# Layer-0 attention, second pass: three quantisations of a tile merged into one over 768 columns in two steps

## The chip, the cores and the metric

The kernel runs on one core of a Trainium2 chip. The time is device microseconds of one execution of the whole program; the time before is the median of three runs.

## The reference, cut to what matters

The program computes four pairs of cross-attention and feed-forward blocks on x of shape 8 x 128 x 256. The change lies in the first attention (`_L0_xattn_ref`), and there in the quantisation of the normalised input before its projections:

```
def _div_clamp_fp8(x, scale):
    y = jnp.clip(x.astype(jnp.float32) / scale, -FP8_MAX, FP8_MAX)
    y = y.astype(jnp.bfloat16).astype(jnp.float32)
    return _fp8_roundtrip(y)

def _fp8_linear_pertensor(x, wq, w_scale, in_scale):
    xq = _div_clamp_fp8(x, in_scale)
    return jnp.einsum('bsi,oi->bso', xq * in_scale, wq) * w_scale
```

This attention works in two halves with 16 query heads each. One takes keys and values from the context, the other takes them from x itself. The half on the context needs x quantised once (for its queries). The half on x needs it three times, with three scales: for queries, keys and values. The mixed heads of both halves are quantised in the same way before the output projection.

## The kernel before, in words

`layer0_attention` runs both halves as one march over 16 tiles of 128 tokens: tiles 0 to 7 are the first pass (on the context), tiles 8 to 15 the second pass ("core" in the code). A tile has 8 steps, one for each projection into a bank of 512 columns: k0, q0, k1, q1, v0, q2, v1, q3. The work of an attention unit is spread over later steps. `march` (line 157) walks the steps in order and, in each step, calls the functions of a list in the order of that list, each at its due steps. Each engine has its own list, written out by hand: TensorE, VectorE (lines 643 to 647), ScalarE and GpSimd (lines 826 and 827). No instruction is moved at run time; engines meet through semaphores alone, and each engine issues in order. Due steps of 8 and more fall into the next tile: step 8 of a tile is step 0 of the next.

Rounding to fp8 is split between two engines. VectorE multiplies by the inverse scale (L569, for the input; L600, for the mixed heads), clips (L552), masks the exponent out of the bf16 number (L554) and makes the rounding step from it (L558). GpSimd adds the step (L776) and subtracts it again (L780). For the mixed heads these operations are 128 x 512 (tiles `y16`, `m16`; result `cat`), for the input 128 x 256 (tiles `yq16`, `mq16`; result `xq`). In the profile names stand without their numbers: `l0a_yq` is `yq16`, `l0a_y` is `y16`, `l0a_mq` and `l0a_m` are the rounding steps.

What happens around the change:

- VectorE, odd steps: variance of the heads (L577), `row_max` of the scores (L590), `normalise` (L585, needs GpSimd's L798 of the step before), then `round_mixed`: L600, L552, L554, L558.
- VectorE, even steps: L577, L594, `normalise` where one is due; in step 2 also `add_to_x` (L607, with L150 and L153 in the second pass); then one `quantise` of the next tile in each of the steps 2, 4, 6 (L569, L552, L554, L558). In the first pass only step 2 has one, since only the queries are quantised. Tile 7 is the first in which three are due, tile 14 the last.
- GpSimd, even steps: `round_mixed` (L776, L780 on 512 columns, for the mixed heads of the step before), `rstd` (L798, 128 x 4, power of -0.5), then `quantise` of the same step (L776, L780 on 256 columns), and in tiles 8 and 9 the preparation of output weights (L810). `rstd` is also due in steps 1 and 3.
- TensorE: in each odd step scores (L410) and mix (L427), in each even step the output projection (L438); `turn` (L401) transposes what L585 wrote; `project` comes last in its step (L392 in the second pass, L384 for keys and values of the first). The projection of k0 of a tile is in step 0, that of q0 in step 1, that of v0 in step 4. It waits for `quant_done` of what it reads: one count for queries, two for keys, three for values.

## Time and profile before

| | |
|---|---|
| median of three runs | 1580.31 us (1577.87 to 1581.35) |
| the profiled execution | 1578.64 us, span 1576.8 us |
| mean granted TensorE clock | 0.975 |
| busy, share of the span | TensorE 93%, VectorE 57%, ScalarE 48%, GpSimd 33% |
| the marched tiles of this attention | from about 28 us to 490 us of the span |
| instructions of the input's quantisation | 32 of each of L569, L552, L554, L558, L776, L780 |

Busy shares over the whole span mix many stages. The change touches one stage only, so what counts are the times inside that stage. The timeline of an engine lists its instructions with their start and length; in square brackets stands the idle time in front of one and who ended it.

### The profile page before, as it was taken

What the parts mean: (1) busy time and instruction counts of PE and PEld (TensorE: products, weight loads), DVE (VectorE), ACT (ScalarE), POOL (GpSimd) and SP (SyncE); (2) the same over time, 40 slices, a digit from 0 to 9 for tenths busy, and PEclk for the clock granted to TensorE, in tenths of its full rate; (3) what the DMA queues carried; (4) which work ended last, traced back from release to release, by engine and by line L of the source; (5) the groups of instructions that cost most, each with busy time, mean ns of one, the idle gap of its engine ahead of it and who ended that gap; (6) DMA issues with size and microseconds to landing.
All of it is one profiled execution on the core that took longest, in us unless ns stands there. A gap on an engine that the chain in (4) does not pass through costs nothing. (4 is left out here: it accounts for less than half of the span.)

```text
span 1576.8 us, 22227 instructions
## 1 busy us (share of the span) xinstructions
PE 1465.0 (93%) x6918; PEld 1044.0 (66%) x6918; DVE 905.4 (57%) x1972; ACT 750.5 (48%) x2052; POOL 526.6 (33%) x510
## 2 busy tenths in 40 slices
PE   4889998899999999999999999999866999989998
PEld 2667777777775555557787979676744666665555
DVE  7787879888875342323465454554684555553322
ACT  3778788788884211110343534343454555554210
POOL 2656567877762000000542425221101333321000
PEclk9999999999999999999999999998977999999999
DMA  4211000200004611112100000002131000011120
GB/s 194 67 52 58 8 5 1 92 1 1 1 1 192 227 48 54 54 47 81 64 1 1 1 1 27 1 0 103 54 137 44 1 1 1 0 29 36 48 67 16
DMA packets 21448, 71.63 MB, mean 45 GB/s; under 512 B 3874, under 2 KB 6306, under 8 KB 18260
## 3 DMA queue, kind: packets, MB, share of 16 engines
q1 hardware_dynamic: 13124, 57.34, 9.8%
q10 hardware_dynamic: 8208, 12.87, 2.7%
q8 instruction: 57, 0.93, 0.3%
q14 instruction: 59, 0.48, 0.1%
HBM read 68.98 MB, written 1.22 MB: 45 GB/s over the span
## 5 line engine op out<-in xcount | busy, mean ns | idle before, releaser
L1130 ACT ACTIVATE l0f_silu<-bank 128x512 f32<-128x512 f32 x48 | 28.6, 597 | 199.9 <-PE bank L1054 189.9
L776 POOL TENSOR_TENSOR l0a_stepped<-l0a_y,l0a_m 128x512 f32<-128x512 bf16 x64 | 76.2, 1190 | 107.0 <-DVE l0a_m L558 106.6
L798 POOL TENSOR_TENSOR l0a_head_rstd<-l0a_head_var,all_minus_half 128x4 f32<-128x4 f32 x96 | 102.3, 1068 | 12.8 <-DVE l0a_head_var L577 12.7
L1233 DVE TENSOR_TENSOR l0f_product<-l0f_silu,bank 128x512 f32<-128x512 f32 x48 | 32.9, 687 | 124.3 <-ACT l0f_silu L1130 124.2
L2247 PE MATMUL bank<-l3a_f_xn_t,all_weights_b 128*128 128x512 f32 (+1 forms) x208 | 93.4, 593 | 0.0
L719 ACT ACTIVATE l0a_work<-bank,l0a_neg_max 128x128 f32<-128x128 f32 x256 | 90.5, 370 | 5.5 <-DVE l0a_neg_max L590 5.3
L401 PE MATMUL bank<-all_ident,l0a_work 128*128 128x128 f32 x384 | 61.5, 284 | 31.4 <-DVE l0a_work L585 30.7
L1066 PEld LDWEIGHTS bank<-all_weights_a,l0f_hidden 128*128 128x128 f32 x384 | 72.9, 190 | 25.2 <-issue 17.0
L1670 DVE TENSOR_TENSOR all_weights_a<-bank,all_cols 128x512 f32<-128x512 f32 x64 | 43.9, 690 | 78.7 <-PE bank L1499 46.2
L1066 PE MATMUL bank<-all_weights_a,l0f_hidden 128*128 128x256 f32 x384 | 88.9, 379 | 0.0
L750 ACT ACTIVATE l0a_work<-l0a_work,l0a_row_inv 128x128 f32<-128x128 f32 x256 | 81.9, 400 | 13.3 <-DVE l0a_row_inv L594 13.3
L410 PEld LDWEIGHTS bank<-l0a_k_t,l0a_q_t 128*128 128x128 f32 x512 | 64.4, 192 | 34.6 <-ACT l0a_q_t L705 27.4
L2514 POOL TENSOR_TENSOR l3a_q_scale<-l3a_q_var,all_minus_half 128x4 f32<-128x4 f32 x32 | 32.3, 1010 | 151.6 <-DVE l3a_q_var L2314 151.6
L780 POOL TENSOR_TENSOR l0a_cat<-l0a_stepped,l0a_m 128x512 fp32r<-128x512 f32 x64 | 77.4, 1209 | 10.5 <-issue 6.2
L691 ACT ACTIVATE l0a_squares<-bank 128x512 f32<-128x512 f32 x96 | 57.5, 599 | 44.5 <-DVE l0a_head_var L577 25.0
L585 DVE TENSOR_TENSOR l0a_work<-bank,l0a_head_rstd 128x512 f32<-128x512 f32 x96 | 65.0, 677 | 21.2 <-POOL l0a_head_rstd L798 21.2
L410 PE MATMUL bank<-l0a_k_t,l0a_q_t 128*128 128x128 f32 x512 | 71.8, 283 | 3.5 <-ACT l0a_q_t L705 2.6
L401 PEld LDWEIGHTS bank<-all_ident,l0a_work 128*128 128x128 f32 x384 | 44.1, 143 | 44.7 <-DVE l0a_work L585 41.3
L577 DVE TENSOR_REDUCE l0a_head_var<-l0a_squares 128x4 f32<-128x516 f32 x96 | 65.7, 684 | 10.6 <-ACT l0a_squares L691 10.5
L1853 ACT ACTIVATE l1a_work<-bank,l1a_exp_bias,l1a_q_scale 128x128 f32<-128x128 f32 x128 | 56.9, 455 | 29.6 <-DVE l1a_exp_bias L1736 29.6
L438 PE MATMUL bank<-l0a_wp_high,l0a_cat 128*128 128x256 f32 x256 | 69.7, 305 | 0.2 <-POOL l0a_cat L780 0.2
L427 PE MATMUL bank<-l0a_probs_t,l0a_values 128*128 128x256 f32 x256 | 66.0, 380 | 0.2 <-ACT l0a_probs_t L726 0.2
(417 smaller groups left out, 3798.2 us busy)
## 6 DMA issues: line engine op xcount, KB each, us to landing
l0f_spread<-l0f_weights ACTq DMA_DIRECT2D x32, 192.0 KB, 2.8
all_weights_a<-in_l_w_q SPq DMA_DIRECT2D x2, 2048.0 KB, 14.4
l0f_spread<-l0f_weights ACTq DMA_DIRECT2D x32, 128.0 KB, 2.8
all_weights_b<-in_l_e_gate SPq DMA_DIRECT2D x1, 3072.0 KB, 10.7
all_weights_a<-in_l_e_up SPq DMA_DIRECT2D x4, 768.0 KB, 7.1
all_weights_a<-in_l_e_down SPq DMA_DIRECT2D x1, 3072.0 KB, 15.5
l3a_spread<-l3f_weights SPq DMA_DIRECT2D x10, 256.0 KB, 3.3
all_weights_b<-in_l_w_qx SPq DMA_DIRECT2D x1, 2048.0 KB, 11.4
```

The source lines that it names most:

```text
L401: mm = pe.transpose(turn_bank[:, h * P:(h + 1) * P], norm_rows[:, m % 2, h * P:(h + 1) * P], res.ident[:])
L410: mm = pe.matmul(score_bank[:, h * P:(h + 1) * P], q_t[:, h * P:(h + 1) * P], k_t[:, a // 2, g * P:(g + 1) * P], start=True, stop=True)
L427: mm = pe.matmul(mix_bank[:, half * 2 * P:(half + 1) * 2 * P], values[:, a // 2, g * P:(g + 1) * P], probs_t[:, half * 2 * P:(half + 1) * ...
L438: mm = pe.matmul(out_bank[:, 0:D], cat[:, a % 2, h * P:(h + 1) * P], part[:, a * HU + h, :], start=(a == 0 and h == 0 and n == 0), stop=(a ...
L577: v.tensor_reduce(head_var[:, m % 2, :], squares[:], X, ALU.add).then_inc(var_ready.sem, 1)
L719: done = act.activation(probs[:, a % 2, h * P:(h + 1) * P], score_bank[:, h * P:(h + 1) * P], ACT.Exp, bias=neg_max[:, a, h:h + 1], accum_ ...
L750: done = act.activation(pr, pr, ACT.Copy, scale=row_inv[:, a, h:h + 1])
L776: done = g.tensor_tensor(stepped[:, 0:n], value, step, ALU.add)
L780: return g.tensor_tensor(out, stepped[:, 0:n], step, ALU.subtract)
L798: g.tensor_tensor(head_rstd[:, m % 2, :], head_var[:, m % 2, :], res.minus_half[:, 0:HU], ALU.pow)\
L1066: mm = pe.matmul(down_banks[t // 2][:, (t % 2) * D:(t % 2 + 1) * D], hidden[:, n % 2, t * P:(t + 1) * P], w_down[:, j, :], start=(j == 0 a ...
L2247: mm = pe.matmul(bank[0:m, :], weights[:, c, col:col + m], f_xn_t[:, c, h * HALF:(h + 1) * HALF], start=(c == 0), stop=(c == KC - 1))
```

## The change

On VectorE `quantise` is replaced by three functions. `quant_scale` does the multiplications (three in the second pass, one in the first) in step 2. `quant_clip` clips all columns with one instruction, in step 2 as well. `quant_step` masks and makes the rounding step, each with one instruction, in step 4. GpSimd still rounds in pieces of 256 columns, now in steps 4, 6 and 8, after a wait for the whole tile's rounding steps. The tile `e16` grows from 512 to 768 columns.

```diff
-        e16 = mem.sb("e16", [BANK], BF16)
+        e16 = mem.sb("e16", [3 * D], BF16)
...
-            def quantise(b, i):
-
+            def quant_width(b):
+                return 0 if b == VTS else 3 * D if b >= TILES else D
+
+            def quant_scale(b, _):
                 b += 1
                 core, t = divmod(b, TILES)
-                if b == VTS or (i > 0 and not core):
+                if quant_width(b) == 0:
                     return
                 v.wait_ge(ln_ready, TILES)
-                quant_done.wait(v, quant_done.at(b - 1, i + 1))
-                part = slice(i * D, (i + 1) * D)
-                v.tensor_tensor(yq16[:, part].rearrange("p (c n) -> p c n", c=KC), ln_t[:, :, t * P:(t + 1) * P],
-                                along(inv_in[:, KC * (core + i):KC * (core + i + 1)], P), ALU.mult)
-                split(yq16[:, part], mq16[:, part], D).then_inc(quant_split.sem, 1 if core else 3)
+                quant_done.wait(v, quant_done.at(b - 1, 3))
+                for i in range(quant_width(b) // D):
+                    v.tensor_tensor(yq16[:, i * D:(i + 1) * D].rearrange("p (c n) -> p c n", c=KC),
+                                    ln_t[:, :, t * P:(t + 1) * P],
+                                    along(inv_in[:, KC * (core + i):KC * (core + i + 1)], P), ALU.mult)
+
+            def quant_clip(b, _):
+                value = yq16[:, 0:quant_width(b + 1)]
+                if b + 1 < VTS:
+                    v.drain()
+                    v.tensor_scalar(value, value, FP8_MAX, -FP8_MAX, ALU.min, ALU.max)
+
+            def quant_step(b, _):
+                n = quant_width(b + 1)
+                if n == 0:
+                    return
+                v.drain()
+                v.tensor_scalar(e16[:, 0:n].bitcast(U16), yq16[:, 0:n].bitcast(U16), 0x7F80, None, ALU.bitwise_and)
+                v.drain()
+                v.tensor_scalar(mq16[:, 0:n], e16[:, 0:n], FP8_MIN_NORMAL, ROUND_3_BITS, ALU.max, ALU.mult)\
+                 .then_inc(quant_split.sem, 3)
...
-                               (round_mixed, later(at_query, 8)), (prepare, range(STEPS)), (quantise, [2, 4, 6]),
+                               (round_mixed, later(at_query, 8)), (prepare, range(STEPS)),
+                               (quant_scale, [2]), (quant_clip, [2]), (quant_step, [4]),
...
-                quant_split.wait(g, quant_split.at(b, i + 1))
+                quant_split.wait(g, quant_split.at(b, 3))
...
-                               (quantise, [2, 4, 6]), (swap_out_low, later(at_query, 11))])
+                               (quantise, [4, 6, 8]), (swap_out_low, later(at_query, 11))])
```

Two places show how instructions move. The first is VectorE in steps 2 to 6 of a second-pass tile. Line numbers shift: L577, L585, L590, L594, L600, L607 and L569 of before are L595, L603, L608, L612, L618, L625 and L571 of the change; of the three instructions that `split` did, L552, L554 and L558 stay for the mixed heads and become L579, L586 and L588 for the input. Before, steps 2 and 3:

```order
L607 SCALAR_TENSOR_TENSOR all_x<-bank,l0a_out_scale,all_x 128x256
L150 BN_STATS all_token_stats<-all_x 128x6
L153 BN_AGGR all_token_moments<-all_token_stats 128x2
L569 TENSOR_TENSOR l0a_yq<-l0a_ln_t,l0a_inv_in 128x256
L552 TENSOR_SCALAR l0a_yq<-l0a_yq 128x256
L554 TENSOR_SCALAR l0a_e<-l0a_yq 128x256
L558 TENSOR_SCALAR l0a_mq<-l0a_e 128x256
L577 TENSOR_REDUCE l0a_head_var<-l0a_squares 128x4
L590 TENSOR_REDUCE l0a_neg_max<-bank 128x4
L585 TENSOR_TENSOR l0a_work<-bank,l0a_head_rstd 128x512
```

The same piece of the change, and behind it step 4:

```order
L625 SCALAR_TENSOR_TENSOR all_x<-bank,l0a_out_scale,all_x 128x256
L150 BN_STATS all_token_stats<-all_x 128x6
L153 BN_AGGR all_token_moments<-all_token_stats 128x2
L571 TENSOR_TENSOR l0a_yq<-l0a_ln_t,l0a_inv_in 128x256 x3
L579 TENSOR_SCALAR l0a_yq<-l0a_yq 128x768
L595 TENSOR_REDUCE l0a_head_var<-l0a_squares 128x4
L608 TENSOR_REDUCE l0a_neg_max<-bank 128x4
...
L603 TENSOR_TENSOR l0a_work<-bank,l0a_head_rstd 128x512
L586 TENSOR_SCALAR l0a_e<-l0a_yq 128x768
L588 TENSOR_SCALAR l0a_mq<-l0a_e 128x768
L608 TENSOR_REDUCE l0a_neg_max<-bank 128x4
```

Step 2 now has three multiplications and one wide clip where it had one multiplication and three narrow instructions. Step 4 has two wide instructions where it had four narrow ones, and step 6 has none.

The second place is GpSimd from step 6 of a second-pass tile to step 2 of the next. L776, L780 and L798 of before are L797, L801 and L819 of the change. Before:

```order
L776 TENSOR_TENSOR l0a_stepped<-l0a_y,l0a_m 128x512
L780 TENSOR_TENSOR l0a_cat<-l0a_stepped,l0a_m 128x512
L798 TENSOR_TENSOR l0a_head_rstd<-l0a_head_var,all_minus_half 128x4 x2
L776 TENSOR_TENSOR l0a_stepped<-l0a_y,l0a_m 128x512
L780 TENSOR_TENSOR l0a_cat<-l0a_stepped,l0a_m 128x512
L798 TENSOR_TENSOR l0a_head_rstd<-l0a_head_var,all_minus_half 128x4
L776 TENSOR_TENSOR l0a_stepped<-l0a_yq,l0a_mq 128x256
L780 TENSOR_TENSOR l0a_xq<-l0a_stepped,l0a_mq 128x256
```

And now:

```order
L797 TENSOR_TENSOR l0a_stepped<-l0a_y,l0a_m 128x512
L801 TENSOR_TENSOR l0a_cat<-l0a_stepped,l0a_m 128x512
L819 TENSOR_TENSOR l0a_head_rstd<-l0a_head_var,all_minus_half 128x4
L797 TENSOR_TENSOR l0a_stepped<-l0a_yq,l0a_mq 128x256
L801 TENSOR_TENSOR l0a_xq<-l0a_stepped,l0a_mq 128x256
L819 TENSOR_TENSOR l0a_head_rstd<-l0a_head_var,all_minus_half 128x4
L797 TENSOR_TENSOR l0a_stepped<-l0a_y,l0a_m 128x512
L801 TENSOR_TENSOR l0a_cat<-l0a_stepped,l0a_m 128x512
```

The pair on 256 columns has left step 2 and stands in step 0 (step 8 of the tile before), between the two `rstd` of steps 0 and 1. Steps 4 and 6 have such a pair in both kernels, but in step 6 it is now the keys' and no longer the values'. TensorE's order is unchanged.

## Rows read from the trace of the kernel before

**Rows 1.** Windows: length; busy PE, PEld, DVE, ACT, POOL; PEclk, DMA share, GB/s.
```profile
203.96:229.81 25.85, 25.85 (x154) 20.58 (x153) 18.98 (x43) 21.25 (x66) 16.87 (x17) 1.00 0.02 6
343.11:369.38 26.27, 24.40 (x153) 20.26 (x152) 22.61 (x51) 21.56 (x68) 19.41 (x20) 1.00 0.00 1
```

**Rows 2.** Timeline of VectorE, tile 11, step 1's end to step 3's end.
```profile
343.11 0.29 DVE L558 TENSOR_SCALAR l0a_m<-l0a_e 128x512 bf16<-128x512 bf16 x1
...
345.97 0.66 DVE L569 TENSOR_TENSOR l0a_yq<-l0a_ln_t,l0a_inv_in 128x256 bf16<-128x256 f32 x1
346.70 0.23 DVE L552 TENSOR_SCALAR l0a_yq<-l0a_yq 128x256 bf16<-128x256 bf16 x1
347.01 0.23 DVE L554 TENSOR_SCALAR l0a_e<-l0a_yq 128x256 uint16<-128x256 uint16 x1
347.31 0.23 DVE L558 TENSOR_SCALAR l0a_mq<-l0a_e 128x256 bf16<-128x256 bf16 x1
347.45 0.68 DVE L577 TENSOR_REDUCE l0a_head_var<-l0a_squares 128x4 f32<-128x516 f32 x1
...
350.79 0.29 DVE L558 TENSOR_SCALAR l0a_m<-l0a_e 128x512 bf16<-128x512 bf16 x1
```

**Rows 3.** The same timeline, steps 4 to 7 of tile 11 and step 1 of tile 12.
```profile
352.77 1.05 DVE L552 TENSOR_SCALAR l0a_yq<-l0a_yq 128x256 bf16<-128x256 bf16 x1
...
357.06 0.29 DVE L558 TENSOR_SCALAR l0a_m<-l0a_e 128x512 bf16<-128x512 bf16 x1
...
357.95 1.00 DVE L569 TENSOR_TENSOR l0a_yq<-l0a_ln_t,l0a_inv_in 128x256 bf16<-128x256 f32 x1
...
363.31 0.30 DVE L558 TENSOR_SCALAR l0a_m<-l0a_e 128x512 bf16<-128x512 bf16 x1
...
367.26 0.69 DVE L585 TENSOR_TENSOR l0a_work<-bank,l0a_head_rstd 128x512 f32<-128x512 f32 x1 [1.04 <-POOL l0a_head_rstd L798]
...
368.64 0.29 DVE L552 TENSOR_SCALAR l0a_y<-l0a_y 128x512 bf16<-128x512 bf16 x1
...
369.38 0.29 DVE L558 TENSOR_SCALAR l0a_m<-l0a_e 128x512 bf16<-128x512 bf16 x1
```

**Rows 4.** Timeline of VectorE, tile 15, which quantises no next tile.
```profile
467.96 0.29 DVE L558 TENSOR_SCALAR l0a_m<-l0a_e 128x512 bf16<-128x512 bf16 x1
...
474.02 0.29 DVE L558 TENSOR_SCALAR l0a_m<-l0a_e 128x512 bf16<-128x512 bf16 x1
```

**Rows 5.** Timeline of GpSimd, tile 11, steps 4 and 6.
```profile
352.57 1.17 POOL L780 TENSOR_TENSOR l0a_cat<-l0a_stepped,l0a_m 128x512 fp32r<-128x512 f32 x1 [0.16 <-DVE l0a_work L585]
...
359.95 1.01 POOL L798 TENSOR_TENSOR l0a_head_rstd<-l0a_head_var,all_minus_half 128x4 f32<-128x4 f32 x1
...
361.93 0.67 POOL L780 TENSOR_TENSOR l0a_xq<-l0a_stepped,l0a_mq 128x256 fp32r<-128x256 f32 x1
```

**Rows 6.** Timeline of TensorE, tile 11 step 4 and tile 12 step 0.
```profile
349.39 0.66 PE L401 MATMUL bank<-all_ident,l0a_work 128*128 128x128 f32 x4 [1.35 <-DVE l0a_work L585]
...
362.34 0.48 PE L392 MATMUL bank<-l0a_wk_high,l0a_xq 128*128 128x512 f32 x1
```

**Rows 7.** Timeline of VectorE, tile 7, step 5.
```profile
240.88 0.68 DVE L585 TENSOR_TENSOR l0a_work<-bank,l0a_head_rstd 128x512 f32<-128x512 f32 x1
```

**Rows 8.** Timeline of GpSimd, tile 7, step 4.
```profile
239.13 1.26 POOL L798 TENSOR_TENSOR l0a_head_rstd<-l0a_head_var,all_minus_half 128x4 f32<-128x4 f32 x1
```

**Rows 9.** Timeline of GpSimd, tile 9, step 0.
```profile
286.53 2.37 POOL L810 TENSOR_TENSOR l0a_wp_low<-all_weights_b,l0a_wp_high 128x1024 fp32r<-128x1024 f32 x1
```

**Rows 10.** The tile l0a_e: durations in ns (min/median/max), then first and last start.
```profile
L558 DVE TENSOR_SCALAR l0a_m<-l0a_e x64: 293/294/297, 61.7 to 484.8; 128x512 bf16<-128x512 bf16 x64
L558 DVE TENSOR_SCALAR l0a_mq<-l0a_e x32: 226/227/229, 24.8 to 439.1; 128x256 bf16<-128x256 bf16 x32
```

**Rows 11.** Timeline of VectorE, tile 10, step 2: a multiplication.
```profile
319.94 0.43 DVE L569 TENSOR_TENSOR l0a_yq<-l0a_ln_t,l0a_inv_in 128x256 bf16<-128x256 f32 x1
```

**Rows 12.** Timeline of ScalarE, tile 12, step 0: the square of k0's bank.
```profile
364.29 0.60 ACT L691 ACTIVATE l0a_squares<-bank 128x512 f32<-128x512 f32 x1 [0.32 <-DVE l0a_head_var L577]
```

More of the change, by code:

```diff
@@ L640, in _ @@
             centre(0)
-            quantise(-1, 0)
+            quant_scale(-1, 0)
+            quant_clip(-1, 0)
+            quant_step(-1, 0)
             low(0)
```

## The prediction

> **What bounds the kernel now.** I read the page for the place, then windows of one tile of each pass, then the timelines of VectorE, GpSimd and TensorE over tile 11.
>
> In a first-pass tile TensorE is busy for all 25.85 us of the window, VectorE for 18.98 [rows 1]. There TensorE is the bound, and what VectorE saves buys nothing. In a second-pass tile TensorE is busy for 24.40 of 26.27 us and VectorE for 22.61 [rows 1]. Nobody is full, so the bound must be found stretch by stretch. I cut the tile at a mark that comes four times: the start of L558 on 512 columns, VectorE's last instruction for the mixed heads, in steps 1, 3, 5 and 7. The marks are 343.11, 350.79, 357.06, 363.31 and 369.38 [rows 2, 3]. So the four turns last
>
> - A (steps 1 to 3): 7.68 us
> - B (3 to 5): 6.27 us
> - C (5 to 7): 6.25 us
> - D (7 to 1): 6.07 us, together 26.27.
>
> Three of them are nearly alike although B and C each hold one quantisation and D none. Tile 15, which quantises nothing, shows why: its turn C lasts 467.96 to 474.02 seen from mark to mark, 6.06 us, with no quantisation beside it [rows 4]. The reader is to see a loop through two engines. GpSimd waits for the mark, adds and subtracts on 512 columns, then does L798. VectorE's L585 of the next odd step waits for that L798 (1.04 us of idle time before 367.26, released by GpSimd) and reaches the next mark 2.12 us later, at 369.38 [rows 3]. From the mark at 363.31 to 367.26 are 3.95 us, so the loop is 3.95 + 2.12 = **6.07 us**. No work taken from VectorE makes a turn shorter than that. Only in A is VectorE's own work longer than the loop: steps 2 and 3 follow without idle time, and TensorE stands idle for 1.35 us before 349.39 for their L585 [rows 6].
>
> There is a second coupling. The clip at 352.77 takes 1.05 us and ends at 353.82; GpSimd's L780 runs from 352.57 to 353.74 [rows 3, 5]. The clip at 346.70, with no such L780 beside it, takes 0.23 us [rows 2]. So a VectorE instruction of this kind stands still until GpSimd's two-input instruction is over. The narrow quantisations of B and C mostly wait inside the 3.95 us that VectorE has to wait anyway.
>
> **Part by part, for a second-pass tile.**
>
> *Turn A.* Before, the quantisation costs 347.45 - 345.97 = 1.48 us in line [rows 2]. The mask and the rounding step leave: 0.30 (347.01 to 347.31) and 0.14 (347.31 to 347.45). Two multiplications come. The one at 345.97 takes 0.66 us in tile 11 and 0.43 us in the same place of tile 10 [rows 2, 11]. Undrained instructions overlap by 0.09 us (0.23 us long, the next 0.14 after it, rows 2), so I take 0.35 us for each of the two. The clip grows from 256 to 768 columns: 226 ns at 256, 293 at 512 [rows 10], so 0.36 us at 768, 0.13 more. It is no longer followed by a drain: about 0.15 less. Sum: -0.44 + 0.70 + 0.13 - 0.15, rounded, **+0.22 us** (between 0 if the new instructions fill an idle gap that I don't see, and +0.8 if the wide clip runs at the multiplication's rate). All of it lies in line, since A has no slack.
>
> The Trainium skill (VectorE: DVE Perf Modes, section "The DRAIN you can't avoid") says that the next VectorE instruction does not start until the pipe of the one before is empty. By that the two multiplications would cost 0.43 us each and A +0.38 us. The 0.14 us between two starts [rows 2] speaks for overlap, so I keep 0.35.
>
> *Turn B.* The quantisation goes, a wide mask and a wide rounding step of 0.36 us each come. They stand beside GpSimd's L780 of the mixed heads, which ends 2.95 us after the mark at 350.79 [rows 2, 5], and are done about 0.75 us behind it at the latest. L590 needs 0.6 us more (0.68 long like L577, less the overlap), so L585 is reached at 4.3 at worst against 3.95 of the loop, at 3.7 if the mask slips in before L780. B is then bound by the loop.
>
> *Turn C.* It loses its quantisation whole. The same loop bounds it.
>
> *Price in B, C and D.* L585 now follows L798 at once, and GpSimd rounds the input right behind L798. From L798's end at 360.96 to the end of the 256-column L780 at 362.60 are 1.64 us [rows 5]. VectorE's clip starts 1.38 us after L585 (367.26, 368.64, rows 3), just inside. A held clip ended 0.08 us after GpSimd (353.82 against 353.74, above). A clip that starts 0.2 us before GpSimd is done is thus some 0.1 us late, an estimate. So each of the three turns lasts 6.07 + 0.1 = 6.17 us: **-0.10** for B, **-0.08** for C, **+0.10** for D, which had no rounding of the input before. Bounds: without any hold -0.20, -0.18 and 0; with GpSimd held up in turn by the wide mask, +0.2 in B.
>
> *GpSimd's queue.* In D the rounding for v (1.64 us) is now ahead of step 1's L798. That L798 then ends about 2.6 us after the first one, and its reader, L585 of step 2, comes 3.1 us after it: 2.12 to the mark, then L558, L577 and L594, 0.9 in line. Half a microsecond of room: nothing. In A GpSimd gets the same 1.64 us free, but it was waiting for VectorE there: nothing.
>
> *TensorE.* k0 of the next tile starts at 362.34 [rows 6]. It now needs GpSimd's rounding of step 6, which ends 362.60 [rows 5], and GpSimd will be in the same place relative to L798. TensorE waits some 0.3 us there. ScalarE's square of that bank starts at 364.29 after 0.32 us of waiting for VectorE's sum L577 [rows 12], not for the bank. That wait covers the 0.3 us, so I cost this at nothing. If the cover is gone (L577 earlier, or the rounding later), it costs up to 0.5 us a tile.
>
> Sum for a steady tile: +0.22 - 0.10 - 0.08 + 0.10 = **+0.14 us**; for tiles 9 to 14 **+0.8 us**.
>
> *Tile 7* has weight preparation on VectorE and is bound by VectorE more widely. In its step 5 L585 starts at 240.88, and L798 ends at 239.13 + 1.26 = 240.39 [rows 7, 8]. B can gain 0.43 us before the loop holds it. I take the same and a little more for C, +0.22 for A: **-0.7 us**. *Tiles 8 and 9* have four L810 of about 2.4 us behind GpSimd's rounding, and in step 0 the rounding for v now comes ahead of one that began at 286.53 [rows 9]. A clip that misses the gap waits for it too. That loses up to 1.2 us there, and the freed step 2 gives about as much back: with A's +0.22 in tile 8, **+0.3 us**, between -1 and +1.5.
>
> *First pass.* Step 2 of each tile gets 0.3 to 0.4 us lighter on VectorE, step 4 heavier, under a TensorE that is never idle: 0.
>
> Total +0.8 - 0.7 + 0.3 = **+0.4 us**. The profiled execution of 1578.64 us becomes 1579.1. It lies 1.67 us below the median of 1580.31, so the median of the change should be about **1581**. A measurement of this kernel tells about 0.2%, 3.2 us, from no change.
>
> **Rivals.**
>
> *Slower: a late key rounding and held turns.* The rounding for k in step 6 is ready only after TensorE wants it. If the 0.3 us wait on TensorE reaches ScalarE's square, L577 and step 1's L798, D grows by up to 0.5 us; if the wide instructions hold GpSimd in B, another 0.2. With the +0.14 that is 0.5 to 0.8 us for each of 8 tiles: +4 to +7, about **1586**. It decides from the point at which k0's bank is full more than 0.32 us later than now. For it: the wait must come. Against it: the 0.32 us of cover, just enough. Wide instructions that don't keep the narrow ones' rate belong here as well (+0.6 us in A, +5 us).
>
> *Faster: the turns have more slack than the loop lets me see.* If no hold comes in B, C and D and A is entered earlier, a tile gains 0.4 to 0.6 us: -3 to -5, about **1576**.
>
> *Faster by far: VectorE is the bound of the whole second pass.* VectorE's quantisation of a tile takes 1.48 us in A and some 2.5 in C (1.00 for the multiplication [rows 3], a held clip like B's 1.05, twice 0.23). In B, with its multiplication at 0.43, it is about 2.0. What stays is 1.7 + 0.75. That is 3.5 us saved for each of 8 tiles, 28 us: **1552**. The Trainium skill (VectorE: DVE Perf Modes, "Rules for kernel authors") advises to minimise the number of VectorE instructions; by it this is the outcome to expect. What speaks against it is that D, without any quantisation, is no more than 0.2 us shorter than B and C.
>
> *The change does nothing at all* would need the instructions to stay; the order of VectorE shows that nine narrow ones became three wide ones.
>
> **How the numbers follow.** Forecast 0.57 (its own range 1578 to 1584); the slower rival 0.25; the faster one with more slack 0.13; VectorE as the bound 0.05. The forecast's edges reach past 0.2% rarely on either side. Faster by over 0.2%: 0.18. Within: 0.56. Slower: 0.26. The range takes in both near rivals, **1575 to 1587**, and leaves out the far one and the tails.
>
> **What would show it.** Right: marks in the changed tile 11 about 7.9, 6.2, 6.2 and 6.2 us apart; VectorE's busy time down by 2 to 3 us in the tile and its idle time up by the same, mostly in front of L603 (the L585 of before), released by GpSimd's L819; the 768-column instructions at 0.36 us; TensorE waiting 0.3 us for `xq` before k0. Wrong: B, C or D clearly below 6.05 us, which would mean that the loop isn't what I take it for; A below 7.5; L819 of step 1 released late by the rounding for v; or a tile period that moves while all four turns read as now.

## The result: a small gain, where no change was forecast

| | before | after |
|---|---|---|
| median of 22 runs | 1578.65 us | 1576.45 us |
| ratio, 95% interval | | 0.9984 (0.9977 to 0.9992) |
| span of the profiled execution | 1576.8 us | 1572.6 us |
| tile 11, mark to mark | 26.27 us | 26.55 us |
| tile 6, mark to mark | 25.58 us | 25.00 us |

The interval makes it 1.3 to 3.6 us faster. The forecast was +0.4 us, and the time lies inside its range of 1575 to 1587, but what moved isn't what I said would move. To find where, I took the marks (the start of L558 on 512 columns) over all tiles. They are far sharper than the median: two profiled executions of one kernel give the same turn within 0.04 us.

First the tile that the prediction was worked out for. VectorE of the changed kernel, tile 11 (L571, L579, L586 and L588 are the input's multiplication, clip, mask and rounding step; L603 is L585 of before, L819 is L798):

```profile
340.34 0.29 DVE L558 TENSOR_SCALAR l0a_m<-l0a_e 128x512 bf16<-128x512 bf16 x1
...
343.20 1.45 DVE L571 TENSOR_TENSOR l0a_yq<-l0a_ln_t,l0a_inv_in 128x256 bf16<-128x256 f32 x3
344.72 0.36 DVE L579 TENSOR_SCALAR l0a_yq<-l0a_yq 128x768 bf16<-128x768 bf16 x1
345.00 0.68 DVE L595 TENSOR_REDUCE l0a_head_var<-l0a_squares 128x4 f32<-128x516 f32 x1
...
348.31 0.29 DVE L558 TENSOR_SCALAR l0a_m<-l0a_e 128x512 bf16<-128x512 bf16 x1
...
350.23 1.24 DVE L586 TENSOR_SCALAR l0a_e<-l0a_yq 128x768 uint16<-128x768 uint16 x1
351.55 0.36 DVE L588 TENSOR_SCALAR l0a_mq<-l0a_e 128x768 bf16<-128x768 bf16 x1
...
354.59 0.29 DVE L558 TENSOR_SCALAR l0a_m<-l0a_e 128x512 bf16<-128x512 bf16 x1
...
358.52 0.69 DVE L603 TENSOR_TENSOR l0a_work<-bank,l0a_head_rstd 128x512 f32<-128x512 f32 x1 [1.86 <-POOL l0a_head_rstd L819]
...
359.91 0.38 DVE L552 TENSOR_SCALAR l0a_y<-l0a_y 128x512 bf16<-128x512 bf16 x1
...
360.73 0.29 DVE L558 TENSOR_SCALAR l0a_m<-l0a_e 128x512 bf16<-128x512 bf16 x1
...
364.68 0.69 DVE L603 TENSOR_TENSOR l0a_work<-bank,l0a_head_rstd 128x512 f32<-128x512 f32 x1 [1.04 <-POOL l0a_head_rstd L819]
...
366.06 0.38 DVE L552 TENSOR_SCALAR l0a_y<-l0a_y 128x512 bf16<-128x512 bf16 x1
...
366.89 0.29 DVE L558 TENSOR_SCALAR l0a_m<-l0a_e 128x512 bf16<-128x512 bf16 x1
```

The turns are A 7.97, B 6.28, C 6.14, D 6.16 against 7.68, 6.27, 6.25, 6.07 [rows 2, 3]. A, C and D came out nearly as forecast: the wide clip and rounding step take 0.36 us, the mixed heads' clip is held for 0.09 (0.38 for 0.29), and in C and D VectorE waits for L819 before L603. B did not get shorter, and its mask takes 1.24 us beside GpSimd.

Now the first pass. VectorE in turn A of tile 6, first the kernel before, then the changed one:

```profile
202.50 0.29 DVE L558 TENSOR_SCALAR l0a_m<-l0a_e 128x512 bf16<-128x512 bf16 x1
...
204.36 1.36 DVE L569 TENSOR_TENSOR l0a_yq<-l0a_ln_t,l0a_inv_in 128x256 bf16<-128x256 f32 x1
205.80 0.23 DVE L552 TENSOR_SCALAR l0a_yq<-l0a_yq 128x256 bf16<-128x256 bf16 x1
206.10 0.23 DVE L554 TENSOR_SCALAR l0a_e<-l0a_yq 128x256 uint16<-128x256 uint16 x1
206.40 0.23 DVE L558 TENSOR_SCALAR l0a_mq<-l0a_e 128x256 bf16<-128x256 bf16 x1
206.54 0.68 DVE L577 TENSOR_REDUCE l0a_head_var<-l0a_squares 128x4 f32<-128x516 f32 x1
...
209.88 0.29 DVE L558 TENSOR_SCALAR l0a_m<-l0a_e 128x512 bf16<-128x512 bf16 x1
```

```profile
200.40 0.29 DVE L558 TENSOR_SCALAR l0a_m<-l0a_e 128x512 bf16<-128x512 bf16 x1
...
202.26 1.35 DVE L571 TENSOR_TENSOR l0a_yq<-l0a_ln_t,l0a_inv_in 128x256 bf16<-128x256 f32 x1
203.69 0.23 DVE L579 TENSOR_SCALAR l0a_yq<-l0a_yq 128x256 bf16<-128x256 bf16 x1
203.83 0.68 DVE L595 TENSOR_REDUCE l0a_head_var<-l0a_squares 128x4 f32<-128x516 f32 x1
...
207.14 0.29 DVE L558 TENSOR_SCALAR l0a_m<-l0a_e 128x512 bf16<-128x512 bf16 x1
```

From the multiplication to L577 (now L595) were 2.18 us and are 1.57: mask, rounding step and one drain are gone. Turn A goes from 7.38 to 6.74 us. There is no idle time of VectorE in it, in either kernel: A is VectorE's own work in the first pass too. (Part of that work is a hold: the multiplication takes 1.36 us, beside GpSimd's L780.) The whole tile by windows from mark to mark (columns as in rows 1), tile 6 before, then tiles 6 and 11 of the changed kernel:

```profile
202.50:228.08 25.58, 25.58 (x152) 20.37 (x151) 18.71 (x42) 20.98 (x67) 16.71 (x16) 1.00 0.02 6
```

```profile
200.40:225.40 25.00, 25.00 (x151) 20.10 (x150) 19.46 (x42) 20.41 (x65) 16.64 (x16) 1.00 0.02 7
340.34:366.89 26.55, 24.28 (x153) 20.38 (x152) 20.89 (x45) 21.41 (x68) 19.53 (x21) 1.00 0.01 1
```

TensorE is busy for 25.58 of 25.58 us and then for 25.00 of 25.00, with the same work. So its busy time stretched with the tile, and "never idle" was no sign of a bound. VectorE's busy time of this tile even rose, from 18.71 to 19.46 us, because the mask in step 4 is held by GpSimd; but that is in turn B, which grew by only 0.07.

The account by marks, the changed kernel against the kernel before: at the first mark, step 1 of tile 1, -1.16 us; from there to tile 7 -1.52; tile 7 -0.84; tile 8 +1.29; tile 9 -0.83; tiles 10 to 14 +0.29, +0.28, +0.32, -0.02, +0.30; the rest of the attention +0.38, nearly all of it in one late turn. Both sides of the first mark need a test.

The late turn and the odd values of single tiles have one source. VectorE of either kernel sometimes stands still for up to 0.43 us with no releaser that the profile shows ("issue"). Where it shows in the second pass, one such stand comes 69 to 75 VectorE instructions after the other, and before the same instruction in both profiled executions of a kernel. In the kernel before, then twice in the changed one:

```profile
372.27 0.18 DVE L153 BATCH_NORM_AGGREGATE all_token_moments<-all_token_stats 128x2 f32<-128x6 f32 x1 [0.43 <-issue]
```

```profile
393.58 0.30 DVE L558 TENSOR_SCALAR l0a_m<-l0a_e 128x512 bf16<-128x512 bf16 x1 [0.43 <-issue]
...
479.40 0.29 DVE L554 TENSOR_SCALAR l0a_e<-l0a_y 128x512 uint16<-128x512 uint16 x1 [0.42 <-issue]
```

From tile 10 on they fall into A of tile 12, B of 13 and C of 14 before, and into B of tile 11 (0.18), D of tile 12, B of tile 14 and one turn behind tile 15 in the changed kernel. Most of them lengthen their turn by 0.27 to 0.36 us. What they are, no run here tells; but a difference of 0.3 us in a single turn has to be checked for them first. The undisturbed tile 10 has A +0.22, B +0.10, C -0.12, D +0.09.

### The profile page after: what moved, and what is told of

The parts are those of the page before. It is cut to its first block and busy times, and to the rows that moved or that the text cites. A ratio compares the mean times of both kernels' runs of the same rounds, so it can differ in the third digit from the quotient of the medians.

```text
span 1572.6 us, 22113 instructions
## 1 busy us (share of the span) xinstructions
PE 1454.6 (92%) x6916; PEld 1038.9 (66%) x6918; DVE 893.3 (57%) x1924; ACT 749.0 (48%) x2052; POOL 526.9 (34%) x510
## 5 line engine op out<-in xcount | busy, mean ns | idle before, releaser
L797 POOL TENSOR_TENSOR l0a_stepped<-l0a_y,l0a_m 128x512 f32<-128x512 bf16 x64 | 76.2, 1191 | 95.8 <-DVE l0a_m L558 94.6
L819 POOL TENSOR_TENSOR l0a_head_rstd<-l0a_head_var,all_minus_half 128x4 f32<-128x4 f32 x96 | 100.5, 1049 | 22.9 <-DVE l0a_head_var L595 22.2
L603 DVE TENSOR_TENSOR l0a_work<-bank,l0a_head_rstd 128x512 f32<-128x512 f32 x96 | 65.1, 678 | 33.6 <-POOL l0a_head_rstd L819 33.4
L801 POOL TENSOR_TENSOR l0a_cat<-l0a_stepped,l0a_m 128x512 fp32r<-128x512 f32 x64 | 78.8, 1231 | 10.5 <-issue 7.8
L595 DVE TENSOR_REDUCE l0a_head_var<-l0a_squares 128x4 f32<-128x516 f32 x96 | 65.6, 684 | 10.7 <-ACT l0a_squares L712 10.3
```

What stands on the lines that cost most here:

```text
L595: v.tensor_reduce(head_var[:, m % 2, :], squares[:], X, ALU.add).then_inc(var_ready.sem, 1)
L797: done = g.tensor_tensor(stepped[:, 0:n], value, step, ALU.add)
L801: return g.tensor_tensor(out, stepped[:, 0:n], step, ALU.subtract)
L819: g.tensor_tensor(head_rstd[:, m % 2, :], head_var[:, m % 2, :], res.minus_half[:, 0:HU], ALU.pow)\
```

## Experiments: which pass, and which half of the change

**The new scheme in one pass alone.** `first_only` uses the three new functions for tiles of the first pass and the old `quantise` for the second; `second_only` is the reverse.

```diff
-   (quant_scale, [2]), (quant_clip, [2]), (quant_step, [4]),
+   (of_new(quant_scale), [2]), (of_new(quant_clip), [2]), (of_new(quant_step), [4]), (of_old(quantise), [2, 4, 6]),
...
-   (quantise, [4, 6, 8]), (swap_out_low, later(at_query, 11))])
+   (of_new(quantise), [4, 6, 8]), (of_old(quantise), [2, 4, 6]), (swap_out_low, later(at_query, 11))])
```

> The new scheme for the tiles of the first pass alone (multiplication and clip in step 2, mask and step in step 4, GpSimd's rounding in step 4); the second pass is quantised as before. Theory (the gain lies in the tiles of the first pass in which VectorE, with the preparation of weights, is the bound, tile 0 above all): the start of L558 of tile 8's step 1 comes some 2.5 to 3.5 us earlier than in the kernel before, as it does in the changed kernel (257.39 to 253.87), and the time is 2 to 3.5 us under the kernel before, about 1576. Rival (the first pass only looks earlier by noise of one profile, the gain comes from the second pass): within 1 us of the kernel before.

Measured: 1576.53 us, ratio 0.9986 (0.9973 to 0.9999). From the first mark to tile 7's it wins 1.54 us, the changed kernel's 1.52, and then runs exactly like the kernel before. At tile 8 it is only 0.95 us ahead, since its first mark came 0.58 us late; expected were 2.5 to 3.5. The part about tile 0 was thus wrong in this profile. The median is 2.35 us lower, as expected, but only 0.95 us of that can be seen in the attention of the profile.

> The new scheme for the eight tiles of the second pass alone (768 columns in two steps, GpSimd in thirds in steps 4, 6, 8); the first pass as before. Theory: tile 7 wins 0.8, tile 8 loses 1.3, tile 9 wins 0.8, tiles 10 to 14 lose about 0.2 each: 0 to +1 us against the kernel before. The marks of tile 11 show a longer turn A (7.9 to 8.0 for 7.68) and a turn D of about 6.16 for 6.07. Rival (the gain comes from the second pass): 2 us or more under the kernel before.

Measured: 1581.11 us, ratio 1.0009 (0.9996 to 1.0022). Up to tile 7 its marks are those of before within 0.1 us, from there on it loses 1.43: -0.82 in tile 7, +1.34 in tile 8, -0.79 in tile 9, and +0.31, +0.28, +0.35, 0.00, +0.37 in tiles 10 to 14, then +0.39. Tile 11's turns are 7.97, 6.27, 6.15, 6.16. The interval takes in no change and the medians alone would not decide, but the marks do: what is gained is gained in tiles 0 to 7, and the second pass costs.

**VectorE's move or GpSimd's.** `gpsimd_four` is the kernel before with GpSimd's first-pass rounding in step 4, and VectorE's quantisation whole in step 2.

```diff
-   (quantise, [2, 4, 6]), (swap_out_low, later(at_query, 11))])
+   (lambda b, i: quantise(b, i) if b >= TILES - 1 else None, [2, 4, 6]),
+   (lambda b, i: quantise(b, i) if b < TILES - 1 else None, [4]), (swap_out_low, later(at_query, 11))])
```

> First pass alone: VectorE's four instructions stay together in step 2 as before, only GpSimd's rounding goes from step 2 to step 4; the second pass as before. If the gain of the first pass comes from GpSimd's rounding leaving step 2, where it holds VectorE's subtraction of the weight halves (L545, 1.61 us beside it in tile 0, 1.22 without), most of it stays: 1.5 to 3 us under the kernel before, tile 0 about 1 us shorter. If it comes from VectorE's mask and step leaving step 2 (some 0.4 us a tile), little stays: within 0.8 us of the kernel before.

Measured: 1579.26 us, ratio 0.9997 (0.9983 to 1.001). A stays at 7.35 us in tile 6, B grows from 6.07 to 6.15, and by marks the first pass loses 0.9 us, 0.6 of it in tile 2. So from tile 1 on GpSimd's move costs a little in most B, and what wins is that VectorE's mask and step leave step 2. Tile 0 is different. There the weight subtraction L545 is no longer held (the kernel before, then `gpsimd_four`):

```profile
41.27 1.61 DVE L545 TENSOR_TENSOR l0a_wq_low<-all_weights_b,l0a_wq_high 128x1024 fp32r<-128x1024 f32 x1
```

```profile
41.38 1.22 DVE L545 TENSOR_TENSOR l0a_wq_low<-all_weights_b,l0a_wq_high 128x1024 fp32r<-128x1024 f32 x1
...
44.99 1.86 DVE L526 TENSOR_TENSOR l0a_w_mean<-l0a_w_mean,l0a_mean_scale 128x8 f32<-128x8 f32 x1
```

The L526 ahead of this one starts at 35.77 in the kernel before, 35.88 in `gpsimd_four` and 35.79 in the changed kernel. From there to this one it is 9.91, 9.11 and 8.51 us (the other two start at 45.68 and 44.30, below). Of tile 0's lead of 1.4 us, 0.8 thus comes with GpSimd's move alone. This execution lost it again, with a first mark at 62.93.

**Two looks at tile 0.** The kernel before and the changed one once more, unchanged.

> The kernel before once more, for a second look at tile 0. Theory (VectorE's own work sets tile 0 up to L526 of its step 4, TensorE's granted clock after it decides how much of a head start is kept): the marks from tile 1 to the end as before within 0.05 us apart; L526 of step 4 at 45.7; the first mark at 61.6 or at about 63, by the clock that TensorE gets between 30 and 60 us.

> The changed kernel once more. Theory: the turns as in the changed kernel within 0.05 us; L526 of step 4 at 44.2 to 44.3, some 1.4 us ahead of the kernel before; the first mark at 60.4 or at about 62.3, by TensorE's clock between 30 and 60 us. Rival (the 1.2 us at the first mark are the change's own and steady): 60.5 again.

Measured: 1576.52 and 1574.83 us in one run each. All turns of the attention repeat within 0.04 us. VectorE reaches L526 of tile 0's step 4 at 45.87 and 44.51, after 45.68 and 44.30 in the first pair. In the kernel before, and in the changed one:

```profile
43.79 0.69 DVE L585 TENSOR_TENSOR l0a_work<-bank,l0a_head_rstd 128x512 f32<-128x512 f32 x1 [0.31 <-POOL l0a_head_rstd L798]
...
45.68 1.41 DVE L526 TENSOR_TENSOR l0a_w_mean<-l0a_w_mean,l0a_mean_scale 128x8 f32<-128x8 f32 x1
```

```profile
42.41 0.68 DVE L603 TENSOR_TENSOR l0a_work<-bank,l0a_head_rstd 128x512 f32<-128x512 f32 x1
...
44.30 1.64 DVE L526 TENSOR_TENSOR l0a_w_mean<-l0a_w_mean,l0a_mean_scale 128x8 f32<-128x8 f32 x1
...
52.60 0.69 DVE L608 TENSOR_REDUCE l0a_neg_max<-bank 128x4 f32<-128x512 f32 x1 [1.14 <-PE bank L410]
```

The lead of 1.4 us is the change's own. How much of it reaches the first mark differs. The changed kernel has it at 60.54 and 60.95, and two kernels that are the same program up to there at 62.28 (`first_only`) and 61.83 (`values_10`, below). The kernel before has it at 61.70 and 62.03, and `second_only`, the same program up to there, at 61.61. On average the four are 0.4 us earlier than the three. The expectations had 61.6 or about 63 for the one kernel and 60.4 or about 62.3 for the other: neither value came again. In `first_only` VectorE waits 2.81 us for the scores instead of 1.14:

```profile
54.34 0.69 DVE L621 TENSOR_REDUCE l0a_neg_max<-bank 128x4 f32<-128x512 f32 x1 [2.81 <-PE bank L410]
```

The granted clock of the two executions in the windows from 40 to 50 and 50 to 60 us, changed kernel first:

```profile
40.00:50.00 10.00, 7.02 (x29) 4.54 (x30) 9.68 (x14) 6.26 (x15) 5.68 (x5) 0.83 0.00 0
50.00:60.00 10.00, 9.98 (x53) 6.97 (x52) 6.30 (x12) 9.09 (x28) 5.38 (x4) 1.00 0.60 225
```

```profile
40.00:50.00 10.00, 6.70 (x29) 4.64 (x30) 9.68 (x14) 6.17 (x14) 5.71 (x5) 0.83 0.00 0
50.00:60.00 10.00, 10.00 (x42) 6.42 (x41) 4.72 (x9) 8.43 (x27) 4.63 (x4) 0.83 0.60 222
```

From 50 us on TensorE had 1.00, its level of 2.4 GHz, in the one and 0.83 in the other, a mean of that and 1.2 GHz. Of all fifteen profiled executions three have 0.83 in that window: `first_only`, `gpsimd_four` and `narrow_468`. From L526 to the first mark they take 17.9 to 18.7 us, the other twelve 16.0 to 17.1. TensorE, busy for 7.0 of the 10 us from 40 to 50, gets its low clock at moments that differ between executions, and a first mark up to 1.7 us later goes with it.

## Experiments: is turn A really the only one

If A is VectorE's own work and B, C and D are the loop, the quantisation should leave step 2 altogether.

**`narrow_468`** is the kernel before with one edit, `(quantise, [2, 4, 6])` made `(quantise, [4, 6, 8])` on both engines. **`narrow_468_keys`** also takes the keys first (parts in the order 1, 0, 2 on both engines, TensorE's counts to match).

> The kernel before with one edit: its narrow quantisations and GpSimd's roundings go from steps 2, 4, 6 to steps 4, 6, 8, so that step 2 has none. Theory (turn A alone is VectorE's own work, in both passes; B, C and D are the loop of 6.07 us plus 0.2 for a narrow quantisation held in it): second pass A 7.7 to about 6.2 (less 1.48), D 6.07 to about 6.27, so 1.2 to 1.3 us less in each of some seven tiles; first pass A 7.38 to 6.1 to 6.3, B 6.07 to 6.27, about 1 us less in the tiles 2, 3, 4 and 6. In all 10 to 14 us under the kernel before, about 1566. Rival (TensorE, which the profile shows busy all the time in the first pass and for 93% in the second, is the bound as soon as A is shorter): first-pass tiles stay at 25.0 us and more, second-pass tiles gain less than 0.5 us, 2 to 5 us in all.

> As narrow_468, and in the second pass the keys are quantised in step 4 and the queries in step 6. TensorE's wait of 0.3 us for xq before k0 goes. Theory (that wait was covered by ScalarE waiting for VectorE): the same time as narrow_468 within 0.5 us. Rival (it reaches L577 and the loop): 0.2 to 0.5 us less in each second-pass tile, 1.5 to 4 us.

Measured: 1573.11 us, ratio 0.996 (0.9942 to 0.9978), and 1576.41 us, 0.998 (0.9961 to 0.9998). `narrow_468` is thus 5.6 us under the kernel before, where 10 to 14 were expected. Its tile 11 has A 6.35, B 6.25, C 6.27 nearly as expected, but D 6.85 for the expected 6.27. The tile gains 0.55 us, not 1.25. D holds two variances (L577 of steps 0 and 1) where B and C hold one, so it has 0.6 us less room. In the first pass A fell to 6.05 in tile 6 and B rose to 6.60. TensorE's window of this tile:

```profile
202.12:226.90 24.78, 24.78 (x149) 19.88 (x148) 18.44 (x42) 20.07 (x63) 16.45 (x16) 1.00 0.02 7
```

Again it is "never idle", now at 24.78 us. The order of the keys changes no turn by more than 0.02 us outside tile 8 (B there +0.21): ScalarE's wait covers TensorE's, as forecast. The two medians differ by 3.3 us all the same, where the stretch from the first mark to the last differs by 0.25: with twelve executions each, the medians don't resolve such a difference.

**`clip_4`** and **`wide_4`** are the changed kernel with its clip, and with clip and multiplications, in step 4.

```diff
-   (quant_scale, [2]), (quant_clip, [2]), (quant_step, [4]),
+   (quant_scale, [2]), (quant_clip, [4]), (quant_step, [4]),
```

> The changed kernel with the clip moved from step 2 to step 4. Theory: A loses the clip, 0.3 to 0.4 us (768 columns) or 0.15 to 0.3 us (256 columns); B has it beside GpSimd's L801, where it waits anyway, and gains 0 to 0.1. Per tile -0.2 to -0.3 in both passes, some 3 us in all under the changed kernel: about 1573. Rival (B is not bound by the loop any more with the wide instructions in it): B grows by the clip's 0.36 to 0.44, and the time is that of the changed kernel within 1 us.

> The changed kernel with the multiplications and the clip in step 4 too, so that all of VectorE's quantisation stands there. Theory: A falls to about 6.2 as in narrow_468. B gets all of it: 3 multiplications at 0.35 to 0.42, clip, mask and step 0.44 each, 2.5 us, and the holds by GpSimd; VectorE's other work of B is about 5, so B is 7.0 to 7.7. A tile of the second pass then lasts 25.4 to 26.2 us against 26.55 in the changed kernel; the time is 2 to 8 us under it, between 1568 and 1575. Rival (merging as such is what costs, wherever it stands): not faster than the changed kernel.

Measured, with ratios to the kernel before: `clip_4` 1574.11 us, ratio 0.9976 (0.996 to 0.9992); tile 11 has A 7.54, B 6.36. One wide clip costs 0.43 us in A and 0.08 in B, and tile 6 falls to 24.72. `wide_4` 1575.92 us, 0.9981 (0.9968 to 0.9995); A 6.47, B 7.49, tile 26.25. That is 0.5 us under the changed kernel where 2 to 8 were expected; by marks it is 1.1. Three multiplications next to GpSimd's L801 and its addition take 2.08 us together, against 1.45 in A above. All of VectorE's quantisation takes 3.31 us there (348.41 to 351.72), and B lasts 1.42 us more than the loop's 6.07. So B has room for about 1.9 us of it, an estimate from these two numbers; the narrow quantisation of `narrow_468`, 2.1 us long in B, makes it 0.2 us longer, which agrees. By the marks the rival, that merging costs wherever it stands, does not hold, though the medians can't tell: what is put into a turn beyond its room lengthens it.

```profile
348.41 2.08 DVE L571 TENSOR_TENSOR l0a_yq<-l0a_ln_t,l0a_inv_in 128x256 bf16<-128x256 f32 x3
350.57 0.36 DVE L579 TENSOR_SCALAR l0a_yq<-l0a_yq 128x768 bf16<-128x768 bf16 x1
```

**Spread over B and C, roundings later.** `split_446` has multiplications and clip in step 4, mask and step in 6, GpSimd in `[6, 8, 10]` with keys first; `split_466` has the clip in step 6.

> The changed kernel with multiplications and clip in step 4, mask and step in step 6, and GpSimd rounding keys in step 6, queries in step 8, values in step 10 (keys first, since k0 needs them in step 0). Theory: A 6.2 (nothing of it in step 2), B with three multiplications and one clip, 1.5 us and a hold, 6.2 to 6.6, C with mask and step 6.2 to 6.3, D with GpSimd's rounding alone 6.15: a second-pass tile 24.8 to 25.3 us against 26.27 in the kernel before, and first-pass tile 6 24.4 to 24.7 against 25.58. In all 9 to 13 us under the kernel before, about 1568. Rival (TensorE or the late rounding takes over as soon as A is at the loop): tiles stay at 25.7 or more, and the time above 1573.

> As split_446, but the clip in step 6 with mask and step. Theory: B 6.1 to 6.3 (multiplications alone), C 6.3 to 6.7 (three wide instructions, the first of them held by GpSimd's L801); the sum within 0.3 us a tile of split_446, about 1568. Rival: C takes the whole of it, 7 us or more, and the tile is above 25.5 us.

Measured: 1592.1 us (ratio 1.0077, 1.0056 to 1.0098) and 1586.7 us (1.0051, 1.0031 to 1.0071). The rival of `split_446` held: its tiles 10 to 14 take 26.8 us and more. B and C stay below 7 us in both (B 6.95 and 6.52, C 6.27 and 6.28 in tile 11), so it wasn't C that took the whole, as the rival of `split_466` had it. TensorE stands in front of q0 until the queries are rounded, and the A behind it is 9.08 us in tile 11 of `split_446` (TensorE, then GpSimd):

```profile
341.98 0.76 PE L392 MATMUL bank<-l0a_wq_high,l0a_xq 128*128 128x512 f32 x1 [3.12 <-issue]
```

```profile
341.21 0.67 POOL L801 TENSOR_TENSOR l0a_xq<-l0a_stepped,l0a_mq 128x256 fp32r<-128x256 f32 x1
```

After these 3.12 us of idle time the granted clock was 0.50 from 342 to 344 us, and a matmul of L392 took 0.63 us for 0.40. Queries as well as keys have to be rounded by step 6; there either order does (`narrow_468_keys`).

**Pairs.** `pair_46` quantises queries and keys as one block of 512 columns in step 4 and the values in step 6; GpSimd rounds in `[4, 6, 8]`.

```diff
-   part = slice(i * D, (i + 1) * D)
...
+   parts = [(0, 1), (2,)][i] if core else (0,)
+   for j in parts:
...
+   part = slice(parts[0] * D, (parts[-1] + 1) * D)
+   split(yq16[:, part], mq16[:, part], len(parts) * D).then_inc(quant_split.sem, len(parts) if core else 3)
...
-   (quantise, [2, 4, 6]),
+   (quantise, [4, 6]),
```

> The kernel before with VectorE's quantisation in step 4 for queries and keys together (512 columns: two multiplications, clip, mask, step) and in step 6 for the values (256 columns); GpSimd rounds in steps 4, 6, 8. Theory (A at 6.2 without quantisation; the slack of B and C is about 1.4 us each; D stays at 6.15 with GpSimd's rounding alone, where narrow_468 had 6.85 for VectorE's quantisation in step 0): B 6.7 to 7.0, C 6.3, D 6.15, a second-pass tile 25.3 to 25.6 us; first pass as in narrow_468. Some 5 to 7 us under the kernel before, about 1572. Rival (B takes more than it gives, as in wide_4's 7.49): no faster than narrow_468.

Measured: 1574.82 us, ratio 0.9982 (0.997 to 0.9993). Tile 11 has A 6.49, B 6.96, C 6.25, D 6.15, in sum 25.85; tile 10 25.55. Turn by turn nearly as expected, and by marks the best of all (4.5 us won after the first mark, `narrow_468` 4.1), though the medians can't tell it from `narrow_468`; the median is 3.1 us under the kernel before, for an expected 5 to 7. `narrow_468`, `clip_4`, `narrow_468_keys`, `wide_4` and `pair_46` all have a ratio of 0.9982 or less, the changed kernel 0.9984. Only for `narrow_468` does the whole interval (up to 0.9978) lie below that value, and even it touches the changed kernel's own (from 0.9977).

**The values' rounding out of step 0.** `values_10` is the changed kernel with GpSimd in `[4, 6, 10]`.

> The changed kernel with GpSimd's rounding of the values in step 10 (step 2 of the next tile, as in the kernel before) for step 8. Theory (the rounding in step 0 is what lengthens turn D by 0.09 us, and, ahead of L810, the turn from tile 8's step 7 to tile 9's step 1 by 1.31 us, 6.86 to 8.17): D back to 6.07 and that turn back to 6.9 to 7.1; A of tile 9 loses what it had won (7.71 back towards 8.85), A of the others stays 0.2 to 0.3 over the kernel before. Time within 1 us of the changed kernel. Rival (the long turn comes from VectorE's wide instructions and not from GpSimd's order): it stays above 8 us.

Measured: 1597.29 us, ratio 1.0123 (1.0102 to 1.0143). D is back at 6.06 to 6.08 us in tiles 10, 11 and 13 and at 6.85 into tile 9: both losses belong to that rounding. (Tile 12's D stays at 6.41: one of the 0.43 us stands lies in it, before the mark at 409.00.) The time is far off, through a wait that I had missed. VectorE's L571 in step 2 must not overwrite the values before they are rounded, and that now happens in the same step: it stands idle 3.21 us.

```profile
356.45 1.10 DVE L571 TENSOR_TENSOR l0a_yq<-l0a_ln_t,l0a_inv_in 128x256 bf16<-128x256 f32 x3 [3.21 <-POOL l0a_xq L801]
```

This is the collision into tile 9 that it removes. VectorE of the changed kernel, then GpSimd (L831 is L810 of before):

```profile
284.43 0.38 DVE L552 TENSOR_SCALAR l0a_y<-l0a_y 128x512 bf16<-128x512 bf16 x1
284.89 2.30 DVE L554 TENSOR_SCALAR l0a_e<-l0a_y 128x512 uint16<-128x512 uint16 x1
287.27 0.30 DVE L558 TENSOR_SCALAR l0a_m<-l0a_e 128x512 bf16<-128x512 bf16 x1
```

```profile
283.99 0.68 POOL L801 TENSOR_TENSOR l0a_xq<-l0a_stepped,l0a_mq 128x256 fp32r<-128x256 f32 x1
284.62 2.42 POOL L831 TENSOR_TENSOR l0a_wp_low<-all_weights_b,l0a_wp_high 128x1024 fp32r<-128x1024 f32 x1
```

The rounding pushes L831 to where the clip slips in ahead of it and the mask does not: a mask of 0.29 us takes 2.30 and ends 0.15 us after L831. Before, L810 began at 286.53 [rows 9], and only the end of it held the clip, for 1.09 us.

## Why the prediction was wrong

**The step that failed is "First pass: ... under a TensorE that is never idle: 0".** The term was -1.5 us for tiles 1 to 6, and VectorE's lead of 1.4 us in tile 0 on top, of which the clock lets some through. The saving itself stood in the same section (step 2 gets 0.3 to 0.4 us lighter on VectorE; the trace gives 0.6). I had found by marks that turn A of the second pass is VectorE's own work and didn't take the marks of the first pass, where A was 7.38 against 6.07 for the other turns of tile 6. I took a busy share of 25.85 of 25.85 us [rows 1] for a bound, in a window that isn't even a tile: from mark to mark tile 6 lasts 25.58. `first_only` and `narrow_468` show the same share at 25.0 and 24.8.

**Turn A, +0.22: right.** The terms written there add up to +0.24. Measured: +0.29 in tile 11, +0.18 to +0.23 in tiles 10, 13 and 14, and -0.11 in tile 12, where the kernel before has a stand of 0.43 us. By the rule of the Trainium skill (VectorE: DVE Perf Modes, "The DRAIN you can't avoid") that the next instruction waits for an empty pipe it would have been +0.38. The section adds that an instruction that is not held starts earlier, which the prediction left out and the trace bears out: L595 starts 0.28 us after a clip of 0.36, and three multiplications of 0.42 each took 1.10 us where nothing held them.

**B -0.10, C -0.08, D +0.10:** measured +0.01, -0.11, +0.09 in tile 11, and +0.10 in B of tiles 10 and 12. B is the term of a steady tile that was off, and its upper bound, GpSimd held up in turn by the wide mask, is what came. In tile 10 the mask slips in ahead of L801, which takes 1.26 us for 1.16; L819 takes 1.12 for 1.01, and L603 starts 4.15 us after the mark and not 3.95 (GpSimd, then VectorE):

```profile
323.45 1.26 POOL L801 TENSOR_TENSOR l0a_cat<-l0a_stepped,l0a_m 128x512 fp32r<-128x512 f32 x1 [0.16 <-DVE l0a_work L603]
```

```profile
325.83 0.69 DVE L603 TENSOR_TENSOR l0a_work<-bank,l0a_head_rstd 128x512 f32<-128x512 f32 x1 [0.30 <-POOL l0a_head_rstd L819]
```

In tile 11 the mask is held behind L801 instead (1.24 us for 0.36). The quiet tiles 10 to 14 lose 1.17 us together in the changed kernel and 1.31 in `second_only`; for tiles 9 to 14 I had +0.8.

**Tile 7, -0.7:** -0.84. **Tiles 8 and 9, +0.3:** +0.46, and with the mechanism named there: +1.31 in one turn, somewhat over the 1.2 given as its upper bound, and -1.14 back in the next A. **GpSimd's queue, nothing:** right for L819. The late turns brought +0.38 that no term had: a stand of 0.42 us that in the changed kernel falls behind tile 15.

The second pass as a whole was forecast at +0.4 and gave +1.17 in the changed kernel, +1.43 in `second_only`. With the first pass's -1.5 in place of the zero, the forecast would have stood at -1.1 without tile 0, and below the kernel before.

**The signs.** VectorE's busy time in tile 11 fell by 1.7 us, not by 2 to 3. Its idle time rose from 1.68 to 4.12 us (the brackets of its timeline), 1.86 us of it in front of L603 in turn C.

**The rivals.** Late keys with held turns: TensorE waits 0.31 us before k0 of tile 12 (at 360.24), and `narrow_468_keys` shows it costs nothing. More slack: no turn of a full tile fell below 6.05. VectorE as the bound of the whole pass: VectorE's busy time in tile 11 fell from 22.61 to 20.89 us and the tile grew; the advice of the Trainium skill (VectorE: DVE Perf Modes, "Rules for kernel authors") to minimise their number bought nothing there.

**What stays open.** By marks the changed kernel wins 0.35 us from the first mark to the last one of the attention (1.16 before it, in that pair), the medians differ by 2.2. The stretch behind the last mark lasts 1092.0 and 1089.7 us in two profiles of the kernel before, 1089.3 and 1089.5 in two of the changed one, 1086.9 to 1093.4 in the others, without a pattern. So 0.35 us and what is kept of tile 0's 1.4 are shown. That is 1.75 us at most, and 0.75 with the mean of 0.4 from four and three executions. The interval of the medians begins at 1.3, and no run tells where more than the marks show would come from.

## What to carry to other kernels

Cut every stage that a change touches by a repeated mark, not only the stage that it is meant for; a turn longer than its neighbours shows whose own work is the bound, and an engine that is busy all the time may only be stretching with it. In a loop through two engines, room is counted turn by turn: here moving instructions out of the one full turn was worth more than making nine into three. And with each moved producer go its readers' deadlines and the buffer's next writer: a rounding two or four steps later cost 8 to 20 us here.

## What the runs showed of the hardware

- VectorE's clip, mask and rounding step on 16-bit values take 0.23 us at 256 columns, 0.29 at 512, 0.36 at 768; 512 more columns cost 0.13 us.
- Beside GpSimd's additions and subtractions of 512 or 1024 columns they are held if they start later, and end after GpSimd by more, the wider they are: 0.08 us at 256 columns (clip at 352.77 [rows 3, 5]), 0.15 at 512 (mask at 284.89), 0.21 at 768 (mask at 350.23, L801 below). The hold works the other way too: L801 took 1.26 us for 1.16 behind a wide mask (323.45). A multiplication of 0.42 us took 1.36 beside L780 (204.36). The power on 128 x 4 does not hold: in `narrow_468` a narrow mask at 363.74 took 0.23 us while L798 ran from 363.54 to 364.55.

```profile
350.09 1.17 POOL L801 TENSOR_TENSOR l0a_cat<-l0a_stepped,l0a_m 128x512 fp32r<-128x512 f32 x1 [0.16 <-issue]
```

- In the second pass VectorE stands still for up to 0.43 us, 69 to 75 instructions apart, without a releaser in the profile and at the same instruction in each execution of a kernel (372.27, 393.58, 479.40); why is open.
- TensorE's granted clock in a stage with idle time differs between executions of the same code (0.83 and 1.00 from 50 to 60 us), and the first mark moved by up to 1.7 us with it, while the turns behind it repeat within 0.04.
